# Mixture-of-experts stage of a one-core kernel: expert slots in 64s instead of 128s, matmul tiles of two 64-row halves

## The reference, cut to what matters

```python
scores = softmax(xf @ Wg); weights, indices = top_k(scores, 4)       # 4096 x 4 = 16384 pairs
for e in range(32):                                                  # pairs of expert e, at most C = 2048
    xg = xf[tok]
    out = (silu(xg @ W1[e]) * (xg @ W3[e])) @ W2[e] * w[:, None]     # 256 -> 128 (twice) -> 256
    y = y.at[tok].add(out)
z = (silu(xf @ Ws1) * (xf @ Ws3)) @ Ws2
```

## Time and profile before

| | |
|---|---|
| time before | 3115.54 us, median of 3 runs (3107.31 to 3118.48) |
| profiled execution | span 3024.1 us; its own device time is not recorded apart from the runs |
| between the median run and the span | 91.4 us, work and waiting outside the first and last instruction |
| busy over the span | PE 90%, ACT 77%, DVE 68%, POOL 24% |

### The profile page before, as it was taken

How to read it: one execution, slowest core, us unless ns; L and a number is a source line. 1 busy time by engine, 2 the same in 40 slices (tenths; PEclk the granted TensorE clock), 3 DMA queues, 4 the chain that set the end, 5 groups by cost and what they waited for, 6 DMA issues and landing times. The chain is left out here.

```text
span 3024.1 us, 60105 instructions
## 1 busy us (share of the span) xinstructions
PE 2726.5 (90%) x16843; PEld 1083.2 (36%) x16844; DVE 2052.2 (68%) x3845; ACT 2319.4 (77%) x3563; POOL 712.5 (24%) x1002
## 2 busy tenths in 40 slices
PE   5799989969999989999999999999999975999972
PEld 5488845512222212222212222211112162888541
DVE  6744458747786777786876886877868867444354
ACT  4644435569999999999999999999999945444320
POOL 1555568620000000000000000000000014555576
PEclk9999999989999999999999999999999985999986
DMA  5555555520010010010010010010001026455644
GB/s 180 151 155 156 152 124 138 138 52 3 5 25 3 5 25 3 5 24 3 5 25 3 5 25 4 4 24 4 3 3 32 3 86 186 151 155 156 115 124 124
DMA packets 132050, 195.29 MB, mean 65 GB/s; under 512 B 22365, under 2 KB 99325, under 8 KB 130429
## 3 DMA queue, kind: packets, MB, share of 16 engines
q1 hardware_dynamic: 104188, 117.00, 13.8%
q0 software_dynamic: 27648, 75.53, 10.3%
HBM read 124.85 MB, written 67.50 MB: 64 GB/s over the span
## 5 line engine op out<-in xcount | busy, mean ns | idle before, releaser
L1683 ACT ACTIVATE RB<-psS 128x1024 f32<-128x1024 f32 x1920 | 1766.1, 1200 | 8.8 <-PE psS L1601 8.6
L1635 PE MATMUL psO<-RB,values 128*32 128x512 f32 x7680 | 1026.1, 606 | 0.5 <-ACT RB L1683 0.5
L1601 PE MATMUL psS<-WE 51*128 51x512 f16 x3840 | 695.3, 387 | 80.6 <-DMA WE<-shift_d 11.2
L1601 PEld LDWEIGHTS psS<-WE 51*128 51x128 f16 x3840 | 174.3, 93 | 1093.9 <-ACT RB L1683 1071.5
L661 POOL DMA_INDIRECT xg<-xn_d,index x320 | 305.0, 953 | 223.0 <-issue 136.5
L685 PE MATMUL psH<-WE,xgt 128*128 x1280 | 341.7, 390 | 0.0
L1547 POOL COPY values<-WE 128x512 f32 x12 | 7.0, 611 | 1319.5 <-PE psO L1635 1319.5
L749 ACT ACTIVATE gate<-psH 128x128 f32<-128x128 f32 x320 | 88.9, 278 | 249.2 <-PE psH L685 249.2
L734 DVE TENSOR_TENSOR hid<-gate,psH 128x128 f32<-128x128 f32 x320 | 92.1, 288 | 261.0 <-ACT gate L749 261.0
L1635 PEld LDWEIGHTS psO<-RB,values 128*32 128x32 f32 x7680 | 151.3, 108 | 277.3 <-issue 245.2
L1699 DVE TENSOR_SCALAR part<-psO 128x512 f32<-128x512 f32 x256 | 171.8, 671 | 114.8 <-PE psO L1601 114.8
(11 more groups left out here) (250 smaller groups left out, 3121.7 us busy)
## 6 DMA issues: line engine op xcount, KB each, us to landing
pair_d<-ob SPq DMA_DIRECT2D x320, 128.0 KB, 1.8
WE<-part_d SPq DMA_DIRECT2D x84, 128.0 KB
xn_d<-ws SPq DMA_DIRECT2D x64, 128.0 KB, 1.7
WE<-in_W SPq DMA_DIRECT2D x2, 4096.0 KB, 23.6
part_d<-raw SPq DMA_DIRECT2D x32, 256.0 KB, 3.0
xg<-xn_d,index POOLq DMA_INDIRECT x320
RA<-in_x SPq DMA_DIRECT2D x8, 512.0 KB, 8.9
head_d<-sums SPq DMA_DIRECT2D x128, 32.0 KB, 1.6
```

The lines of the kernel that those rows point to most:

```text
L1601: return pe.matmul(ps, K[r][rows, kt * P:(kt + 1) * P], Q[r][rows, at:at + BLK], start=True, stop=True)
L1635: last = pe.matmul(psO[g % 2][32 * j:32 * (j + 1), :], values[:, r, j % 2, kt, :], weights, start=(kt == 0), stop=(kt == KT - 1))
L1683: act.activation(probs[n % RING][:, half * 2 * BLK:(half + 1) * 2 * BLK], psS[m % HELD][:, :], ACT.Exp, scale=SCALE).then_inc(sem("exped"), 1)
```

## The change

Slots are rounded up to 64 per expert instead of 128. A tile still has 128 slots, but its two halves can belong to two experts. The fixed number of tiles is then `NJ` = 128 + 16 = 144. `tile_expert` holds an expert for each half. The first half's weights are read from `WE` as before; VectorE copies the second half's weights (128x768 fp32) from `WE` into `mate`, four buffers, once per tile. Each up or down product becomes two of 64 stationary columns, one for the first half (array columns 0 to 63, output partitions 0 to 63) and one for the second. The transposes stay 128x128. TensorE's and VectorE's programs of this stage are written out for all 144 tiles, with no loop, and the experts are read into registers four tiles at a time.

```diff
@@ constants
-NJ = T * TOPK // P + E
+SUB = 64
+SUBS = P // SUB
+NJ = T * TOPK // P + E // SUBS
+NSUB = NJ * SUBS
@@ experts, TensorE
+                def turn(j):
+                    pe.wait_ge(gathered[j % U], 16 * (1 + j // U) + L * 16 * NJ // U)
+                    for c in range(DC):
+                        last = pe.transpose(psX[j % 2][:, c * P:(c + 1) * P], xg[:, j % U, c * P:(c + 1) * P], ident[:, :])
+                    last.then_inc(sem("x_turned"), 1)
+                def halves(j, w):
+                    return (WE[:, expert[j], w], mate[:, j % U, w])
+                def up(j):
+                    expert[j] = pe.snap(owner[j // U % 2][j % U], min_val=0, max_val=E - 1)
+                    pe.wait_ge(sem("mated"), j + 1)
+                    pe.wait_ge(sem("xgt_ready"), j + 1)
                     for c in range(DC):
-                        last = pe.matmul(psH[(s + 1) % 2][:, :], xgt[:, (s + 1) % 2, c * P:(c + 1) * P],
-                                         WE[:, e, c * 2 * H:(c + 1) * 2 * H], start=(c == 0), stop=(c == DC - 1))
+                        for n, weights in enumerate(halves(j, slice(c * 2 * H, (c + 1) * 2 * H))):
+                            last = pe.matmul(psH[j % 2][n * SUB:(n + 1) * SUB, :], xgt[:, j % 2, c * P + n * SUB:c * P + (n + 1) * SUB],
+                                             weights, start=(c == 0), stop=(c == DC - 1))
+                def down(j):
+                    pe.wait_ge(sem("hidt_ready"), j + 1)
+                    if j >= 2:
+                        pe.wait_ge(sem("ob_ready"), j - 1)
+                    for n, weights in enumerate(halves(j, slice(DC * 2 * H, WCOLS))):
+                        last = pe.matmul(psO[j % 2][n * SUB:(n + 1) * SUB, :], hidt[:, j % 2, n * SUB:(n + 1) * SUB],
+                                         weights, start=True, stop=True)
-                skewed(pe, NJ, U, step)
+                for j in range(-2, NJ + 1):
+                    if j + 2 < NJ:
+                        turn(j + 2)
+                    if 0 <= j + 1 < NJ:
+                        up(j + 1)
+                    if 0 <= j < NJ:
+                        turn_hidden(j)
+                    if 0 <= j - 1 < NJ:
+                        down(j - 1)
@@ experts, VectorE
+                def mated(j):
+                    if j % U == 0:
+                        v.reg_load(owner, tile_expert[0:1, 1, j:j + U])
+                    e = v.snap(owner[j % U], min_val=0, max_val=E - 1)
+                    if j >= U:
+                        v.wait_ge(sem("down"), j - U + 1)
+                    v.tensor_copy(mate[:, j % U, :], WE[:, e, :]).then_inc(sem("mated"), 1)
+                for j in range(-2, NJ):
+                    if j + 2 < NJ:
+                        turned(j + 2)
+                        mated(j + 2)
+                    if 0 <= j + 1 < NJ:
+                        hidden(j + 1)
+                    if j >= 2 and (j - 2) // U < NW:
+                        weigh((j - 2) // U, (j - 2) % U)
-                skewed(v, NJ, U, step, weigh)
```

More of the change, by code:

```diff
@@ L223, in ffn @@
         with ExitStack() as late:
+            tile_expert = sb(f"tile_expert{L}", [1, SUBS, NJ], I32, late)
             slot_key = sb(f"slot_key{L}", [P, NW, E], F32, late)
@@ L642, in experts @@
         match = sb(f"match{L}", [P, 2, TOPK, E], F32, c)
+        mate = sb(f"mate{L}", [P, U, WCOLS], F32, c)
         psX = [pb(f"psX{i}_{L}", [P, D], F32, c) for i in range(2)]
@@ L703, in _, with fetch @@
-                skewed(pe, NJ, U, step)
+                owner = [[pe.alloc_register(f"owner{n}_{u}_{L}") for u in range(U)] for n in range(2)]
+                expert = {}
+                def fetch(group):
+                    pe.reg_load(owner[group % 2], tile_expert[0:1, 0, group * U:(group + 1) * U])
+                def turn(j):
[3 more added lines that the diff above has]
+                    last.then_inc(sem("x_turned"), 1)
@@ new lines, in halves @@
+                def halves(j, w):
[4 more added lines that the diff above has]
+                    pe.wait_ge(sem("xgt_ready"), j + 1)
+                    for c in range(DC):
+                        for n, weights in enumerate(halves(j, slice(c * 2 * H, (c + 1) * 2 * H))):
+                            last = pe.matmul(psH[j % 2][n * SUB:(n + 1) * SUB, :], xgt[:, j % 2, c * P + n * SUB:c * P + (n + 1) * SUB],
+                                             weights, start=(c == 0), stop=(c == DC - 1))
+                    last.then_inc(sem("up"), 1)
@@ new lines, in turn_hidden @@
+                def turn_hidden(j):
+                    pe.wait_ge(sem("hid_ready"), j + 1)
+                    pe.transpose(psG[j % 2][:, :], hid[:, j % 2, :], ident[:, :]).then_inc(sem("h_turned"), 1)
+                def down(j):
[5 more added lines that the diff above has]
+                                         weights, start=True, stop=True)
+                    last.then_inc(sem("down"), 1)
+                    del expert[j]
@@ L722, in weigh, with turned, hidden @@
                         v.wait_ge(sem("summed"), i + 1)
[L724 to L735, removed]
-                skewed(v, NJ, U, step, weigh)
+                owner = [v.alloc_register(f"mate_owner{u}_{L}") for u in range(U)]
+                def turned(j):
+                    v.wait_ge(sem("x_turned"), j + 1 + U)
+                    if j >= 2:
+                        v.wait_ge(sem("up"), j - 1)
+                    v.tensor_copy(xgt[:, j % 2, :], psX[j % 2][:, :]).then_inc(sem("xgt_ready"), 1)
+                def mated(j):
[5 more added lines that the diff above has]
+                    v.tensor_copy(mate[:, j % U, :], WE[:, e, :]).then_inc(sem("mated"), 1)
+                def hidden(j):
+                    v.wait_ge(sem("gated"), j + 1)
+                    if j >= 2:
+                        v.wait_ge(sem("h_turned"), j - 1)
+                    v.tensor_tensor(hid[:, j % 2, :], gate[:, j % 2, :], psH[j % 2][:, H:], ALU.mult)\
+                     .then_inc(sem("hid_ready"), 1)
+                v.wait_ge(sem("we_in"), 16 * 5)
+                for j in range(-2, NJ):
[6 more added lines that the diff above has]
+                        weigh((j - 2) // U, (j - 2) % U)
             @block.scalar
```

24 lines of the change are left out of this document (13 added, 11 removed).

## The result

| | median, us | range | ratio to before, same chip |
|---|---|---|---|
| before | 3111.43 | 3105.82 to 3118.48 | |
| changed | 3199.30 | 3188.77 to 3201.74 | 1.028, 95% interval 1.0257 to 1.0303 |

The change makes the kernel slower by 88 us, where +90 was predicted (3206, range 3170 to 3270).

A forecast was written before the change was run, and what follows sets the result against it. TensorE's stream was taken to bound the experts stages. Four width switches per tile would lengthen the two stages by 92.5 us, route would save 4, about +90 on 3115.5: 3206 us, range 3170 to 3270.

The forecast's parts named there:

- What bounds the kernel: Experts stages: TensorE's stream, 1.63 us per tile without holes between groups; the stages average 1.73 per tile.
- The halves side by side: Up and down products: both 64-column halves run simultaneously, so the stream per tile stays 1.63 us.
- Rival B: Up and down products: halves run one behind the other, turn 3.50 us, +462, time 3573 us; chance 0.03.
- The price of a change of width: TensorE, per tile: four switches between 128 and 64 columns cost 0.58 us, bounds 0.54 and 0.68; turn 2.21.
- A: TensorE's switches cost nothing: turn near 1.65 us, time 3044, or 3106 if VectorE binds at 1.87; chance 0.09.
- C: TensorE's switches are dearer, with more exposed loads and late semaphores: turn 2.42 us, time 3264 us; chance 0.12.
- VectorE's copy at nothing: Experts stages: the weights copy takes 0.55 us per tile (bounds 0.5 and 0.95), hidden under TensorE's turn.
- Rival D: GpSimd's gathers come late, blocked by the copy; decides from 0.96 us per tile, 3501 us at 2.0; chance 0.04.
- rival E: TensorE's clock falls to 1.2 GHz in the experts stages: turn about 3.9 us, +575, time 3690 us; chance 0.03.
- The sum: Experts stages: filling 6.4, 143 turns of 2.21, emptying about 1.5; 323.9 us each, 647.8 against 555.3, +92.5.
- The narrower one-hot rows of `route`: Route: `at_tile` 10% narrower saves 4 us, at most 8, lower bound nothing.
- the 91.4 us: Whole kernel: difference between profiled span 3024.1 and median 3115.5 us, taken as lying around the span and kept unchanged.

The follow-up runs named there:

- e2: Changed kernel with products of 128 stationary columns again, both halves using the first half's expert, copy still made and waited for; 3041.1 us, ratio 0.976 to the kernel before.
- e9: Changed kernel with a tile's transposes and up-product halves interleaved, so the width changes six times per tile; 3203.0 us, ratio 1.058 to the kernel before.
- e3: Changed kernel without VectorE's weights copy and the wait for it, second half always with expert 0; 3212.3 us, ratio 1.030 to the kernel before.
- e10: Changed kernel with VectorE's copy of the weights made twice per tile; 3125.2 us, ratio 1.033 to the kernel before.
- e6: Kernel before (160 tiles of one expert each) with TensorE's and VectorE's loops written out, nothing else; 3012.2 us, ratio 0.995 to the kernel before.
- e1: Kernel before, unedited, run again for a profile beside its own time; 3121.43 us, span 3119.7.
- e4: Changed kernel with TensorE's order regrouped (both kinds of transposes, then up, then down), two width changes per tile; 3173.9 us, ratio 1.017 to the kernel before.
- e8: Changed kernel, same order, down product at 128 columns again and up products still halved, two width changes per tile; 3032.6 us, ratio 1.0019 to the kernel before.
- e7: Changed kernel in two-tile blocks, weights copy split, gathered tiles transposed a block earlier, up before down products; 2999.5 us, ratio 0.9906 to the kernel before.

## Why the prediction was right

*What bounds the kernel.* TensorE's stream. e2 kept everything but the narrow products and had the 1.63 us turn again (mean 1.66), with 16 tiles fewer: 0.976.

*The halves side by side.* Right, and the strongest inference from the row of L1635 in the earlier trace rows: pairs start within 0.01 us and follow at 0.215. Rival B is out.

*The price of a change of width.* 0.58 us per tile predicted, 0.59 measured (2.22 - 1.63). Its parts are as they were read from the earlier trace rows: holes of 0.09, 0.06 of load ahead of transposes, 0.05 ahead of 64 columns, the value that had no row. The straight line over 0, 2, 4 and 6 changes, and e9 above all, show that it is the changes that are paid, not the narrow passes. Rivals A and C are out. In all these runs the 128-column work beside a change is a transpose; what a change between a 128-column product and 64 columns costs was not run. The drain that the Trainium skill names ("TensorEngine Tiling (Array Packing)", Tiling Modes) holds for 128 against 64 columns too; the runs put 0.15 us on it, with the exposed load (0.09 without).

*VectorE's copy at nothing.* Right: 0.552 us against 0.55. e3 without it is no faster, e10 with two of them costs 0.3%. I called the cover thin at a turn of 1.63; e2 ran that turn with the copy, so it was enough there too.

*The gathers.* Rival D did not come, and its mechanism is there in small. The gather takes 953 ns on average without the copy (e3, and the kernel before) and 1041 to 1046 with it (the changed kernel, e2, e9), whatever the turn. The mean hides two kinds:

```profile
304.86 0.55 DVE L758 COPY mate<-WE 128x768 f32 x1
305.27 0.96 POOL L665 DMA_INDIRECT xg<-xn_d,index  x1 [1.27 <-PE psX L682]
...
307.40 0.56 DVE L758 COPY mate<-WE 128x768 f32 x1 [0.17 <-issue]
307.50 1.31 POOL L665 DMA_INDIRECT xg<-xn_d,index  x1 [1.07 <-PE psX L682]
```

Of the changed kernel's 288 gathers, 200 start about 0.4 us behind a copy's start, when it is nearly done, and take 0.96. Where VectorE first reads four experts, at every fourth tile, its copy comes 0.3 later; the gather then starts 0.1 behind it, and 66 such gathers take 1.30. That is 0.35 for one in four, far from the 0.96 in each tile at which it would decide. The lock-out that "SBUF — State Buffer" of the Trainium skill describes would have this sign; here it was never five-fold.

*The clock.* 1.00 and 0.99 in the two stages, as before; rival E is out.

*The sum.* 323.9 per stage predicted, 324.1 and 323.9 measured. Three things were off. The narrower one-hot rows of `route` were to bring 4 us and brought nothing that can be told: the first transposes start at 127.6 us, and at 127.6 in e6 too, which has the wide rows. The instruction takes 323 ns with 144 columns, 321 with 160, so in this range its time does not go by width, while I had scaled it.

```profile
L620 DVE TENSOR_SCALAR at_tile<-iota_h,hi_f,number 128x144 f16<-128x144 f16 x256 | 70.2, 323 | 5.6 <-PE psI L499 3.3 <-issue 1.9
```

I took the 91.4 us between the profiled span and the median as lying around the span. They did not (e1): the profiled execution was shorter. And with it went the stages that I subtracted: 555.3 in that profile, 562.3 in e1's, so that the stages grew by 86 and not by 92.5. The forecast survived because it was made as a difference within the experts stages; that the total came within 2 us is in part luck, since the 4 us of `route` that did not come and the 7 us of the base have opposite signs, and the runs of one kernel lie up to 13 us apart.

*One statement on what the profile would show was wrong.* TensorE's busy share in the stage was to fall below 100%. The stretch of the kernel after shows 319.8 of 320 us:

```profile
130.00:450.00 320.00, 319.81 (x2143) 147.07 (x2143) 192.20 (x534) 128.92 (x427) 151.38 (x174) 1.00 0.38 116
```

The modelled end of a pass lies 0.16 behind its stream, which covers a hole of 0.09. Busy time could not show this loss at all; starts in the timeline did.

## What to carry to other kernels

Splitting a matmul into column halves is free only while TensorE stays at one width: each change between 128-column transposes and 64-column products costs 0.15 us here, so before cutting tiles count the changes, and group work of one width (two tiles per block made the same cut a gain of 0.9%, 0.4% over the kernel before with its loops written out). When work is moved to save such changes, look for the ring that it closes: up product, silu, `hid` and transpose took 2.07 us round in e4 and ate more than half of the saving. To judge a full engine, add up starts in the timeline, since "busy" hides holes shorter than the 0.16 us by which a pass's modelled end lies behind its stream.

## What the runs showed of the hardware

- The price of width changes is additive: 0.149 to 0.150 us each over 2, 4 and 6 per tile (turns 1.628, 1.927, 2.225 and 2.527 us, each the median over the first stage of the time between the starts of successive transposes of `hid`, in e2, e8, the changed kernel and e9). Every such step adds one change each way; in the timeline the two ways cost about alike, 0.09 + 0.06 toward 128 columns and 0.09 + 0.05 toward 64.
- An fp32 copy of 0.55 us on VectorE lengthened the GpSimd gather beside it from 0.95 to 1.30 us when the gather started 0.1 us behind it, and by 0.01 when it started 0.4 us behind it. A second copy right behind the first added 0.01 to the mean. In e7, with the copy cut into pieces of 0.42 and 0.29 us at other places, the mean gather took 0.96. So when the two meet counts, and not only how much VectorE copies; which part of the gather waits was not separated.
- The combine stages, whose program is the same in all runs, took about 235 and 180 us on two chips and 283 and 218 on a third, 85 us of 3100, with the experts stages nearly alike. Comparing across chips would have hidden or doubled this change's effect.
